# Cross attention in a decoder layer: scores with the keys stationary, softmax on turned 32x32 blocks, values one step later

## What is computed

```
q = (query @ Wq + bq).reshape(B, L, NKV, G, HDIM)      # 32 heads of 128
k_, v_ = jnp.split(kv @ Wkv + bkv, 2, axis=-1)         # 8 key/value heads
scores = jnp.einsum('blkgd,bmkd->bkglm', q, k) * scale
attn = jax.nn.softmax(scores, axis=-1)
o = jnp.einsum('bkglm,bmkd->blkgd', attn, v).reshape(B, L, NHEAD * HDIM)
return o @ Wo + bo
```

## Time and profile before

| | us |
|---|---|
| median of 3 runs | 2822.52 |
| lowest, highest | 2820.04, 2824.1 |
| span of the profiled execution | 2819.6 |
| cross attention loop, first score matmul to that of step 63 | 1649.40 to 2721.53 |

### The profile page before, as it was taken

The page is one execution under the profiler, slowest core; times in us unless marked ns, Lnnn a source line. Parts: engine busy times, 40 slices in busy tenths (PEclk is TensorE's granted clock), DMA queues, the critical chain, the costliest instruction groups (busy, mean ns, idle before and its releaser), DMA issues.

```text
span 2819.6 us, 64777 instructions
## 1 busy us (share of the span) xinstructions
PE 2769.3 (98%) x27264; PEld 2437.1 (86%) x27264; DVE 1821.9 (65%) x3253; ACT 1504.1 (53%) x3207; POOL 1512.3 (54%) x1299
## 2 busy tenths in 40 slices
PE   7999999999999999999999999999999999999997
PEld 6888889888888888888888888888888888888886
DVE  6667666676666667666666765655555556555577
ACT  5566665566666566566556644443334444443345
POOL 6887887888776666676666732222224222222125
PEclk9999999999999999999999999999999999999999
DMA  5223313423334231333122221111112111111111
GB/s 172 86 83 103 98 60 102 108 67 91 107 92 137 82 89 47 85 82 88 52 82 81 66 83 42 35 47 36 42 38 60 46 42 34 42 34 42 31 30 60
DMA packets 91483, 197.74 MB, mean 70 GB/s; under 512 B 20665, under 2 KB 21305, under 8 KB 89145
## 3 DMA queue, kind: packets, MB, share of 16 engines
q1 hardware_dynamic: 71480, 154.80, 19.5%
q10 hardware_dynamic: 17664, 34.61, 3.6%
q0 software_dynamic: 2048, 4.20, 0.5%
HBM read 176.78 MB, written 16.78 MB: 69 GB/s over the span
## 4 chain that ended last, share of the span: by engine, by line
PE 93%; DVE 3%; ACT 1%; issue 1%; POOL 1%; DMA 0%; SPq 0%; ACTq 0%
PE big L1786 35%; PE bank L1786 28%; PE big L1858 14%; PE bank L1878 13%; PE big L1878 2%; PE bank L1779 1%; DVE P L1375 0%; DVE nmx L1369 0%; PE big L1779 0%; POOL ptl L779 0%; DVE stat L1714 0%; DVE z L1486 0%; POOL oTl L784 0%; DVE xTl L514 0%; ACT P L943 0%
## 5 line engine op out<-in xcount | busy, mean ns | idle before, releaser
L779 POOL TENSOR_TENSOR ptl<-P,pth 128x576 fp32r<-128x576 f32 x512 | 724.9, 1435 | 237.7 <-ACT pth L952 237.0
L943 ACT ACTIVATE P<-big,nmx 128x576 f32<-128x576 f32 x512 | 378.1, 739 | 404.6 <-DVE nmx L1369 402.2
L1375 DVE STREAM_TRANSPOSE P<-P 128x576 f32<-128x576 f32 x512 | 387.7, 767 | 149.7 <-ACT P L943 147.6
L1878 PE MATMUL bank<-pth,v 32*128 32x256 f32 x4608 | 425.7, 281 | 5.7 <-DVE xacc L1397 1.4
L1878 PE MATMUL big<-pth,v 32*128 32x256 f32 x4608 | 425.8, 282 | 0.0
L1878 PEld LDWEIGHTS bank<-pth,v 32*128 32x128 f32 x4608 | 383.5, 187 | 18.3 <-issue 15.6
L1369 DVE TENSOR_REDUCE nmx<-big 128x1 f32<-128x576 f32 x512 | 373.1, 747 | 3.5 <-PE big L1858 1.4
L952 ACT ACTIVATE pth<-P 128x576 fp32r<-128x576 f32 x512 | 347.5, 682 | 51.6 <-DVE P L1375 51.1
L1878 PEld LDWEIGHTS big<-pth,v 32*128 32x128 f32 x4608 | 363.5, 187 | 0.0
L1878 PE MATMUL bank<-ptl,v 32*128 32x256 f32 x2304 | 350.2, 278 | 0.0
L1878 PE MATMUL big<-ptl,v 32*128 32x256 f32 x2304 | 330.5, 278 | 0.0
(11 more groups left out here) (270 smaller groups left out, 7880.2 us busy)
## 6 DMA issues: line engine op xcount, KB each, us to landing
rall<-kept_r ACTq DMA_DIRECT2D x64, 512.0 KB, 3.7
raw<-in_wo SPq DMA_DIRECT2D x64, 256.0 KB, 3.3
raw<-in_xWq SPq DMA_DIRECT2D x64, 256.0 KB, 2.7
raw<-in_xWo SPq DMA_DIRECT2D x64, 256.0 KB, 2.6
raw<-in_wq SPq DMA_DIRECT2D x62, 256.0 KB, 2.9
v<-kept_v SPq DMA_DIRECT2D x24, 448.0 KB, 7.6
v<-kept_v SPq DMA_DIRECT2D x68, 128.0 KB, 3.3
raw<-in_xWkv SPq DMA_DIRECT2D x32, 256.0 KB, 2.8
```

The source lines that it names most:

```text
L779: pool.tensor_tensor(third_columns(ptl, i), blocks_of(i), f(third_columns(pth, i)), ALU.subtract).then_inc(p_low(i), 1)
L943: act.activation(P[:, i % PSLOTS, :].rearrange("p (k n) -> p k n", k=2), ps_s[i % 2][:, :, 0:HALF], ACT.Exp, bias=nmx[:, i % 8:i % 8 + 1], ...
L1375: dve.transpose(P[:, i % PSLOTS, :], P[:, i % PSLOTS, :]).then_inc(p_turned(i), 1)
L1878: m = pe.matmul(ps_o[a][:, 0:256], v[r, s, l, :], p[r, lo:hi + 1:hi - lo, block_of(b), :, :], start=first, stop=final)
```

## The change

- Scores: the keys (64 high and 64 low columns side by side) are now stationary and the queries of two pairs of heads are the moving operand, 256 columns, twice (high and low query). PSUM rows are now keys: rows 0 to 63 and 64 to 127 hold the two shares, in swapped places for odd and even sequences (`key_high`, `key_low`), and two sequences fill the 128 partitions of P2.
- Softmax: P2 holds the scores with keys on partitions. DVE turns P2 in 32x32 blocks, so that 32 keys of a query stand along a row, takes maxima and sums of 32, exchanges them between partitions 32 apart with four small copies (`swap_halves`) and combines them; POOL multiplies, and DVE turns P2 back. p2h is then copied by ACT from P2 and p2l made by POOL. The four PE transposes and the bank `ps_tp` are gone; the bank is the second one for projections.
- Order: `values2(n-1)` runs on PE behind `score2(n)`; the high and low parts of its outputs (`out2_hi`, `out2_lo`) and of the value rows made in the step before (`next_value_hi`, `next_value_lo`) move to the next step's softmax. Both projections run behind the two query blocks. In the last step `linear` and the turned tiles stand before the projections.

PE, step 37 (g = 9, s = 1), before. L1786 is every product, L1779 a transpose; xk keys, xq queries, xwo and xo output weights and outputs, yT and wqT tokens and query weights, xp and xv probabilities and values. Names read moving operand, stationary operand.

The diff, cut:

```diff
-        ps_tp = bank[0][:, :]
-        ps_w = bank[1][:, :]
+        ps_w = [bank[1][:, :], bank[0][:, :]]
...
+            mx2, mxo = sb("mx2", [128, 16], F32, two)
...
+        def by_parity(ap):
+            return ap.rearrange("p (b q) o i -> p b (q o) i", q=2)
+        def key_high(s):
+            return by_parity(k2[:, 4 * s:4 * s + 4, :, :])[:, :, 0:4:3, :]
+        def key_low(s):
+            return by_parity(k2[:, 4 * s:4 * s + 4, :, :])[:, :, 1:3, :]
+        def key_columns(ps):
+            return ps[:, 0:256].rearrange("p (b q i) -> p b q i", q=2, i=64)
...
+                gate.wait_ge(tile_hi, ("p2", n))
+                pool.tensor_tensor(p2l[:, :], flat(P2[:, :, :]), f(p2h[:, :]), ALU.subtract).then_inc(
+                    p_low((2, n)), 1)
...
+            def out2_hi(n):
+                gate.wait_ge(pv_done, ("v2", n))
+                if n >= 1:
+                    gate.wait_ge(wo_done, (2, n - 1, 1))
+                h = 40 + n // 4 % G
+                for par in range(2):
+                    act.activation(o2h[:, :, 64 * par:64 * par + 64],
+                                   ps_ov[par].rearrange("p (x i) -> p x i", i=64), ACT.Identity,
+                                   bias=bqk[:, h:h + 1]).then_inc(o_hi((2, n, par)), 1)
+            def next_value_hi(n):
+                g, s = n // 4, n % 4
+                if g % 2 == 1 and g + 1 < GG:
+                    value2_hi(g + 1, s)
...
                last = n == STEPS - 1
-                for bp in range(2):
-                    gate.wait_ge(s_done, (2, n, bp))
+                for par in range(2):
+                    own, other = 64 * par, 64 * (1 - par)
+                    gate.wait_ge(s_done, (2, n, par))
                     if n >= 1:
-                        gate.wait_ge(tile_tr, ("p2", n - 1))
-                    act.activation(P2[:, bp].rearrange("p (x k) -> p x k", k=64),
-                                   ps_sc[:, bp, :].rearrange("p (x a k) -> p x a k", a=2, k=64)[:, :, 1, :],
-                                   ACT.Copy).then_inc(sb_done((n, bp)), 1)
-                for tt in early_x3(n):
-                    tile_high("x3", tt)
+                        gate.wait_ge(p_low, (2, n - 1))
+                    act.activation(flat(P2[:, :, :])[own:own + 64, :], ps_sc[other:other + 64, par, :], ACT.Copy).then_inc(
+                        sb_done((n, par)), 1)
+                if n >= 1:
+                    out2_hi(n - 1)
+                    next_value_hi(n - 1)
+                for m, j in units(n)[:1]:
+                    query2_hi(m, j)
+                if last:
+                    for tt in early_x3(n):
+                        tile_high("x3", tt)
                 gate.wait_ge(max_done, (2, "sub", n))
                 act.activation(flat(P2[:, :, :]), flat(P2[:, :, :]), ACT.Exp, scale=SCALE).then_inc(
                     exp_done((2, n)), 1)
                 for tt in tiles_at(g, s):
                     weight2("ctx", tt)
-                for m, j in units(n):
+                for m, j in units(n)[1:]:
                     query2_hi(m, j)
                 for tt in tiles_at(g, s):
                     tile_high("x2", tt)
-                gate.wait_ge(tile_tr, ("p2", n))
+                if n == 0:
+                    key2_hi(0, 3)
+                    value2_hi(0, 3)
+                gate.wait_ge(p_turned, (2, n))
                 if n >= 1:
                     gate.wait_ge(pv_done, ("v2", n - 1))
-                act.activation(p2h[:, :], ps_tp, ACT.Copy).then_inc(tile_hi(("p2", n)), 1)
-                if n == 0:
-                    key2_hi(0, 3)
+                act.activation(p2h[:, :], flat(P2[:, :, :]), ACT.Copy).then_inc(tile_hi(("p2", n)), 1)
...
+            def next_value_lo(n):
+                g, s = n // 4, n % 4
+                if g % 2 == 1 and g + 1 < GG:
+                    value2_lo(g + 1, s)
...
+            def swap_halves(dst, src, signal, event):
+                for a in range(4):
+                    b = a ^ 1
+                    dve.tensor_copy(dst[32 * a:32 * a + 32, :], src[32 * b:32 * b + 32, :]).then_inc(signal(event), 1)
             for n in range(STEPS):
                 g, s = n // 4, n % 4
                 work = blocks_at(g, s)
                 last = n == STEPS - 1
-                for bp in range(2):
-                    gate.wait_ge(sb_done, (n, bp))
-                    ab = ps_sc[:, bp, :].rearrange("p (x a k) -> p x a k", a=2, k=64)
-                    dve.tensor_tensor(P2[:, bp].rearrange("p (x k) -> p x k", k=64), ab[:, :, 0, :],
-                                      P2[:, bp].rearrange("p (x k) -> p x k", k=64), ALU.add).then_inc(
-                                          sm_done(("sum", n, bp)), 1)
-                if n == STEPS - 3:
-                    tile_low("x3", early_x3(n)[0])
+                rows2 = flat(P2[:, :, :])
+                for par in range(2):
+                    own = slice(64 * par, 64 * par + 64)
+                    gate.wait_ge(sb_done, (n, par))
+                    dve.tensor_tensor(rows2[own, :], ps_sc[own, par, :], rows2[own, :], ALU.add).then_inc(
+                        sm_done(("sum", n, par)), 1)
                 gate.wait_ge(sm_done, ("sum", n, 1))
-                dve.tensor_reduce(mx2[:, :], pv, AX.X, ALU.max).then_inc(max_done((2, "max", n)), 1)
+                dve.transpose(flat(P2[:, :, :]), flat(P2[:, :, :])).then_inc(sm_done(("rows", n)), 1)
+                gate.wait_ge(sm_done, ("rows", n))
+                dve.tensor_reduce(mx2[:, :], pv, AX.X, ALU.max).then_inc(max_done((2, "half", n)), 1)
+                gate.wait_ge(max_done, (2, "half", n))
+                swap_halves(mxo, mx2, max_done, (2, "other", n))
+                gate.wait_ge(max_done, (2, "other", n))
+                dve.tensor_tensor(mx2[:, :], mx2[:, :], mxo[:, :], ALU.max).then_inc(max_done((2, "max", n)), 1)
                 gate.wait_ge(max_done, (2, "max", n))
-                dve.tensor_tensor(pv, pv, mx2[:, :].unsqueeze(2).to_broadcast([128, 8, 64]), ALU.subtract).then_inc(
+                dve.tensor_tensor(pv, pv, mx2[:, :].unsqueeze(2).to_broadcast([128, 16, 32]), ALU.subtract).then_inc(
                     max_done((2, "sub", n)), 1)
-                if n < STEPS - 4:
-                    add_out2(n - 1, 0)
-                for tt in early_x3(n)[:1]:
-                    if n != STEPS - 3:
+                if n >= 1:
+                    out2_lo(n - 1)
+                    next_value_lo(n - 1)
+                if last:
+                    for tt in early_x3(n):
                         tile_low("x3", tt)
                 gate.wait_ge(exp_done, (2, n))
-                dve.tensor_reduce(sm2[:, :], pv, AX.X, ALU.add).then_inc(sm_done(("row", n)), 1)
-                gate.wait_ge(sm_done, ("row", n))
+                dve.tensor_reduce(sm2[:, :], pv, AX.X, ALU.add).then_inc(sm_done(("half", n)), 1)
+                gate.wait_ge(sm_done, ("half", n))
+                swap_halves(smo, sm2, sm_done, ("other", n))
+                gate.wait_ge(sm_done, ("other", n))
+                dve.tensor_tensor(sm2[:, :], sm2[:, :], smo[:, :], ALU.add).then_inc(sm_done(("both", n)), 1)
+                gate.wait_ge(sm_done, ("both", n))
                 dve.reciprocal(sm2[:, :], sm2[:, :]).then_inc(rec_done((2, n)), 1)
-                for tt in early_x3(n)[1:]:
-                    tile_low("x3", tt)
-                if n >= STEPS - 4:
-                    add_out2(n - 1, 0)
-                if n >= STEPS - 2:
-                    statistics(pairs2(g, n - STEPS + 2), 2)
-                for m, j in units(n):
+                for m, j in units(n)[:1]:
+                    query2_lo(m, j)
+                if last:
+                    z_out(0)
+                gate.wait_ge(p_norm, (2, n))
+                dve.transpose(flat(P2[:, :, :]), flat(P2[:, :, :])).then_inc(p_turned((2, n)), 1)
+                for m, j in units(n)[1:]:
                     query2_lo(m, j)
                 for tt in tiles_at(g, s):
                     tile_low("x2", tt)
-                gate.wait_ge(tile_hi, ("p2", n))
-                dve.tensor_tensor(p2l[:, :], ps_tp, f(p2h[:, :]), ALU.subtract).then_inc(tile_lo(("p2", n)), 1)
                 if n == 0:
                     key2_lo(0, 3)
+                    value2_lo(0, 3)
+                add_out2(n - 1, 0)
...
-                for bp in range(2):
-                    for p in range(2):
-                        for bo in range(2):
-                            i = 2 * bp + bo
-                            kk = flat(k2[:, 4 * s + i])
-                            c0 = 256 * p + 128 * bo
-                            end = p == 1 and bo == 1
-                            at = Q_PLACE[(n // 2, p, n % 2)]
-                            products(ps_sc[:, bp, c0:c0 + 128], [(q2h[:, at, i, :], kk), (q2l[:, at, i, :], kk)],
-                                     s_done if end else None, (2, n, bp))
...
```

(48 more changed lines are left out.)

104 lines of the change are left out of this document (36 added, 68 removed).

## The result

| | us |
|---|---|
| before, median (lowest, highest) | 2823.31 (2820.04, 2824.91) |
| changed kernel, median (lowest, highest) | 2968.61 (2958.89, 2974.99) |
| ratio, 95% interval | 1.0516 (1.0494 to 1.0538) |
| profiled execution: span before, after | 2819.6, 2957.1 |
| first score matmul of the loop to that of step 63: before, after | 1072.1, 1205.5 |

The change makes the kernel 5.2% slower. The direction was forecast, the size was not: 2896 us was named and 2848 to 2940 given as the range; the result is 29 us above its upper end. Of the 137.5 us on the span, 133.4 lie in the cross attention loop up to step 63, 6.8 behind it, and 2.7 were gained ahead of it. The profiled execution is the fastest of the four, at a mean granted clock of 0.971; the three others had 0.966 to 0.969, and the median lies 9.7 us above it. What follows is read from the profiled one.

The account below looks back on a forecast made before the run. PE, busy 98% of the span, was taken as the bound. Terms -79 + 77 + 2 + 20 + 5 + 16 + 32 = +73 on the 2819.6 us span gave 2893, with 2.9 for the median 2896 us; range 2848 to 2940.

Parts of the forecast that it names:

- What PE loses: Cross attention loop: faster scores and no transposes take 1.23 us a step off PE, 64 times, -79 us.
- rival D: Scores: 256-column matmuls with strided moving operand stream no faster, 50 us of gain missing, 2946 us; chance 0.02.
- Wait 1: Odd groups' second query block: PE waits 2.75 us for the value rows' low part, 28 steps, +77 us.
- Wait 2: Fourth output weight block's late load delays the next step's output low parts: +20 us even groups, +2 odd.
- Wait 3: Layer norm statistics in steps 9 and 41 delay the next sums, +5 us; tail steps 61 to 63, +16.
- Costed at nothing: POOL's low part of the probabilities, ready at about T = 12.2 (13.0 odd groups), and other covered parts: 0 us.
- The clock: Half clock on PE after some 38 waits, 1.7 us each, bounds 0 and 65 us; half taken, +32.
- Rival B: PE's clock falls at nearly every wait: +106 us, 2929 us; chance 0.2.
- rival A: Same PE waits, but the clock stays up: +41 us, 2864 us; chance 0.22.
- Rival C: Second query block: value bank wait hidden by overlap, low part done by T = 6.0; -38 us, 2785 us; chance 0.06.

Follow-up runs that it names:

- Experiment 2: Changed kernel with 13 unread 512-column matmuls on PE between the two query blocks of the 28 waiting steps; 2925.0 us, ratio 1.0359.
- Experiment 5: Changed kernel with Experiment 3's edit, values back in their own step, output and value row parts at its end; 2859.2 us, ratio 1.0123.
- Experiment 1: Changed kernel with value rows' parts made first: ACT's high part ahead of the outputs', DVE's low part behind the two sums; 2848.6 us, ratio 1.0089.
- experiment 4: Changed kernel with the edits of Experiment 1 and Experiment 3 together; 2788.7 us, ratio 0.9885 to the kernel before.
- Experiment 3: Changed kernel with the fourth output weight block's split moved into the next step, behind output and value row parts; 2901.5 us, ratio 1.0271.

## Why the prediction was wrong, step by step

- **What PE loses, 1.23 us a step.** Right: clean steps were forecast at 17.38 and 14.49 and took 17.37 and 14.49 to 14.50. The scores at 0.12 us each rule out rival D.
- **Wait 1, the value bank.** The place, the cause and the number of waits (28) were right. Size: 79 forecast with the 2 us of the weights' delay, 92.9 measured. By items, forecast and measured end in T: sums 2.6 and 2.72; turn 3.35 and 3.46; maximum 4.1 and 4.19; exchange 4.52 and 4.98; combined 4.75 and 5.19; subtraction 5.45 and 5.91; output low parts 6.8 and 7.35; value low part 7.4 and 7.95. The mis-sized term is the four copies: 0.42 taken, 0.76 measured. Both bounds had been written down; I took the lower because the copies don't wait for each other, and that reason was wrong. The Trainium skill's page "VectorE: DVE Perf Modes", section on the TRN2 errata, by which each small instruction pays its fixed latency, led to the estimate of 0.17 a copy; the trace agrees nearly (0.17 in duration, 0.19 from start to start), and the row of two aggregates should not have been set above it.
- **Beside each wait.** A step with only the wait of 3.02 us is 3.24 longer than a clean one. Most of the 0.2 us is in how the wait is counted: it runs from the end of the last matmul's row, 0.39 after that row's start, while a full stream has its next start after 0.23 (T = 4.82, not 4.98). Experiment 2's step, with PE filled, is as long (20.61), so this is no price of running empty. Over some 40 waits it comes to 8 us, which stand in no term of the forecast.
- **Wait 2, the fourth output weight block.** Mechanism right, 20 forecast, 28.3 measured for the same eight places (3.07 to 3.85 each and 5.02 in step 1): the output low parts are late by the copies as well.
- **Wait 3.** Steps 10 and 42, behind the layer norms, 2.86 each (5 forecast, 5.7). Steps 61 to 63: waits of 5.15, 7.21 and 1.07, then 1.51, 1.71 and 2.50, so 19.2 where 16 was forecast. A wait of 3.1 in step 0 was not forecast.
- **Costed at nothing.** The probabilities' low part held in the changed kernel: PE waited 0.2 us for it in all. Experiment 5, where it is wanted earlier, shows it at T = 12.5 against 12.2.
- **The clock.** This is the step that failed: "I take half", 32 us, for a fall at 19 of 38 waits at 1.7 us. What remains of the 137.5 us after -79 for the matmuls and +160 for the waits and their 0.2 us is about 56. The price of a fall was right, the number was not. 21 of the 28 value steps show a granted clock under 1.00, and 12 of the 13 other steps with a long wait, so four in five; of the forecast's 38 places 30 did, not 19. By length, less the clean step, the wait and 0.2, a fall costs 1.3 to 1.7 us in most of the 21 and 2.5 to 2.9 in four, 37 us in all and 1.8 on the mean; experiment 2 took 37 off these steps. The low clock reaches from the wait through the query block behind it. Rival B had this as its case, and its 65 us for the clock are nearer than the 32; rival A, the clock left up, is refuted for most waits. The Trainium skill's page "TensorE: Matmul & The Clock Gate", section "Why this matters for your kernels", advises against pauses of about this length. The forecast's 2.75 us lay just under that, so it served rival A; the measured waits, 3.02 us and more, lie at it or above, and the trace agrees with the advice in 21 of the 28 steps, not in the other 7.

In sum, the forecast's 73 against 137.5: clock 24 too little, value bank 14, wo2 8, the 0.2 us beside the waits 8, the rest 10 (layer norms, step 0, tail and small waits). The range failed at its upper end since it combined rival B with the lower value of the chain. With the upper bound of the copies (0.8), so 0.4 more at each of the 36 waits of both kinds, and rival B's clock the same working gives some 2943. What would still be missing are the 0.2 us beside each wait, the waits of step 0 and the small ones, and the rest of both chains.

Rival C named its deciding point, a value low part at T = 6.0. Experiment 1 does by order what C thought would happen by overlap: the low part ends at T = 3.44. But C kept the wait for the weight block, as experiment 1 does, and that kernel takes 2848.6 us where C had 2785, since the clock still falls at the waits left and the output low part is late. That experiment 4, with this wait gone too, comes out at 2788.7 is chance.

Left open: why one wait of 3.02 us lowers the clock and the next one doesn't. Steps 46 and 54 have the same program text and the same wait. Experiment 3 shows that it isn't fixed by the step, since the falls moved; no run here tells by what rule. The length of the wait sets the odds. In steps 1 to 62 of the changed kernel and the seven experiments, sorted by the longest wait of PE in the step, none of 65 steps with 1.0 to 1.9 us shows a fall, one of 4 with 2.4, 5 of 10 with 2.9, 58 of 79 with 3.0 to 3.7 and all 23 with more.

## What to carry to other kernels

When a drain is moved into a busier place, ask which PSUM bank it frees and who is next in the ring for that bank: here moving one subtraction of 0.68 us forward again from the last of eight places got back 120 of the 145 us. Cost a wait of PE as the wait as counted, 0.2 us beside it, and, once it is past 3 us, 1.8 us of half clock in four cases of five. Count small DVE instructions one by one at their full 0.19 us; and before a reordered algorithm is given up, move the parts that somebody waits for ahead of those that nobody does.

## What the runs showed of the hardware

- A single wait of PE of 3.0 us between full streams lowers the granted clock from 2.4 to 1.2 GHz in most cases, not in all: 21 of 28 steps with such a wait (3.0 to 3.8 us, one of 6.9). Filling it with matmuls that nobody needs made the kernel 43.6 us faster. Waits of 1.0 to 1.9 us lowered it in none of 65 steps.
- Copies of 32x16 float32 on DVE take 0.17 us each, and 0.19 from one start to the next, also with no wait between them (1.55 us for eight). A 32x32 turn of 128x512 takes 0.71.
- Score matmuls of 256 columns come 0.12 us apart; the old ones of 128 columns took 0.11 each (1.74 us for 16). Twice the columns cost next to nothing; that is 0.78 of the 1.23 us that a clean step gained, and the four transposes that went are most of the rest.
